# Projections that read the recurrence's output in its own column order, without ACT's copy sorted by tile

## The reference

```
xn = layernorm(x)
# branch 1, a gated linear recurrence
xc    = causal_conv(xn, 4 taps) + conv_b
r, i  = sigmoid(xc @ W_r.T + b_r), sigmoid(xc @ W_i.T + b_i)
a     = sigmoid(log_a) ** (8 r)
h_t   = a_t * h_(t-1) + sqrt(clip(1 - a_t^2)) * i_t * xc_t     # along the 256 tokens
o     = h @ W_out.T
att   = o * rsqrt(mean(o^2) + 1e-6) * gamma
# branch 2, a mixture of 8 experts, each with room for 512 tokens
p, e  = max and argmax of softmax(xn @ Wr);  rank of the token among those of its expert
y     = p * (relu(xn_e @ W1[e]) @ W2[e])        # dropped if the rank is over 511
out   = x + att + y
```

## Time and profile before

| what | value |
|---|---|
| time, median of 3 executions | 130.73 us (130.49 to 130.87) |
| span of the profiled execution, first to last instruction | 128.8 us |
| granted TensorE clock, mean over the span | 0.958 |
| busy: PE, weight loads, DVE, ACT, POOL | 82%, 70%, 79%, 77%, 66% |
| copies sorted by tile on ACT (L796) | 8, together 8.2 us |
| projections (L640) | 64 matmul records, together 8.8 us |

### The profile page before, as it was taken

One profiled execution on the slowest core, in us unless ns is written; L12 is line 12 of the kernel. 1 busy time (PEld: TensorE's weight loads), 2 busy tenths in 40 slices (PEclk: granted clock), 3 DMA queues, 4 the chain that ended last, 5 costly groups with the idle time before them and its releaser, 6 DMA issues.

```text
span 128.8 us, 2229 instructions
## 1 busy us (share of the span) xinstructions
PE 106.2 (82%) x711; PEld 89.9 (70%) x711; DVE 101.8 (79%) x238; ACT 99.6 (77%) x219; POOL 84.6 (66%) x109
## 2 busy tenths in 40 slices
PE   3999999999799999999999997999997999700000
PEld 3999976672379779789879987898697899600000
DVE  5398998999699999979614489999999975973690
ACT  3299792888589589789689999999999799823560
POOL 8987774078788787778777877888787878700000
PEclk9999999999999999999999999999999999998555
DMA  2966964892456365312611711111110111149995
GB/s 85 383 247 173 405 244 173 318 380 66 103 169 181 80 209 139 118 53 56 209 41 41 219 51 41 61 37 41 52 57 25 60 43 61 41 108 302 325 372 215
DMA packets 8234, 19.27 MB, mean 150 GB/s; under 512 B 1689, under 2 KB 1945, under 8 KB 8224
## 3 DMA queue, kind: packets, MB, share of 16 engines
q1 hardware_dynamic: 5424, 13.70, 31.5%
q0 software_dynamic: 2080, 4.19, 11.2%
q10 hardware_dynamic: 720, 1.25, 2.6%
HBM read 10.82 MB, written 8.39 MB: 149 GB/s over the span
## 4 chain that ended last, share of the span: by engine, by line
PE 60%; DVE 9%; DMA 8%; ACT 8%; issue 5%; POOL 4%; POOLq 1%; SPq 1%; DVEq 0%; ACTq 0%
PE bank L624 17%; PE bank L609 6%; PE bank L611 6%; PE bank L610 6%; DMA dec<-y_rows 4%; PE bank L640 4%; PE bank L453 3%; PE bank L561 3%; PE bank L442 3%; POOL xn_tok L405 3%; DMA xn_tok<-xn_rows,idx_in 2%; ACT xc L796 2%; PE bank L594 2%; PE bank L563 2%; PE bank L562 2%
## 5 line engine op out<-in xcount | busy, mean ns | idle before, releaser
L405 POOL DMA_INDIRECT xn_tok<-xn_rows,idx_in x32 | 33.7, 1054 | 14.4 <-issue 9.4
L417 POOL DMA_INDIRECT y_rows<-xn_tok,idx_out x32 | 33.5, 1047 | 9.7 <-issue 9.1
L624 PE MATMUL bank<-w_raw,h_sb 128*128 128x128 f32 x256 | 29.9, 275 | 0.0
L624 PEld LDWEIGHTS bank<-w_raw,h_sb 128*128 128x128 f32 x256 | 29.2, 192 | 0.0
L786 ACT ACTIVATE h_sb<-bank 128x512 f32<-128x512 f32 x32 | 18.8, 598 | 2.5 <-PE bank L611 0.6
L609 PE MATMUL bank<-xg_hi,w_hi 128*128 128x512 f32 x32 | 13.2, 412 | 0.0
L611 PE MATMUL bank<-xg_hi,w_lo 128*128 128x512 f32 x32 | 12.6, 393 | 0.0
L610 PE MATMUL bank<-xg_lo,w_hi 128*128 128x512 f32 x32 | 12.5, 391 | 0.0
L1021 DVE SCALAR_TENSOR_TENSOR xc<-xnT,par,xc 128x1020 f32<-128x1020 f32 (+2 forms) x9 | 11.5, 1277 | 0.3
L640 PE MATMUL bank<-par,xc 128*128 128x128 f32 x64 | 8.8, 280 | 2.2 <-ACT xc L796 1.3
L1061 DVE TENSOR_TENSOR_SCAN xnT<-dec,bank 128x256 f32<-128x256 f32 x16 | 10.1, 674 | 0.3
(11 more groups left out here) (143 smaller groups left out, 243.2 us busy)
## 6 DMA issues: line engine op xcount, KB each, us to landing
w_raw<-in_weights SPq DMA_DIRECT2D x8, 512.0 KB, 3.9
y_rows<-sca SPq DMA_DIRECT2D x4, 512.0 KB, 5.9
dec<-y_rows SPq DMA_DIRECT2D x8, 256.0 KB, 5.7
x_tok<-in_x SPq DMA_DIRECT2D x3, 512.0 KB, 5.9
xn_rows<-xn_tok SPq DMA_DIRECT2D x3, 512.0 KB, 3.6
out<-dec SPq DMA_DIRECT2D x4, 256.0 KB, 3.1
out<-dec ACTq DMA_DIRECT2D x4, 256.0 KB, 2.9
x_tok<-in_x SPq DMA_DIRECT2D x2, 256.0 KB, 3.5
```

The lines of the kernel that those rows point to most:

```text
L405: g.indirect_dma_start(gathered[:, s * D:(s + 1) * D], None, xn_rows, bass.IndirectOffsetOnAxis(ap=idx_in[:, s:s + 1], axis=0)).then_inc(g ...
L417: g.indirect_dma_start(y_rows, bass.IndirectOffsetOnAxis(ap=idx_out[:, s:s + 1], axis=0), gathered[:, s * D:(s + 1) * D], None, bounds_che ...
L624: last = mm(tile_of(e, s), h_sb[:, k * CAP + s * P:k * CAP + (s + 1) * P], w_raw[:, e, F + k * D:F + (k + 1) * D], start=(k == 0), stop=(k ...
```

## The change

ACT's `order` is gone, with its semaphore and the `ordered` buffer. `project` and `fold` read the scan's output `hs` itself. Of each unit's 512 columns, tile i takes every fourth one, from column i on: the stationary operand has a step of 4 fp32 elements, 16 bytes. The matmuls wait for the scan instead of for the copy.

```diff
-        ordered = xc
...
-        ACT_AT = {0: "decay0 gates1", 1: "gates2", 2: "square2 gates3", 3: "scale0", 4: "order0 order1 scale2",
-                  5: "order2 scale3 squares1 order3", 6: "order4 order5 squares3", 7: "squares6 squares7"}
+        ACT_AT = {0: "decay0 gates1", 1: "gates2", 2: "square2 gates3", 3: "scale0", 4: "scale2", 5: "scale3 squares1", 6: "squares3",
+                  7: "squares6 squares7"}
...
-                     5: "lead7 squares2", 6: "order6 order7 squares4 squares5"}
+                     5: "lead7 squares2", 6: "squares4 squares5"}
...
             def project(n):
-                pe.wait_ge(order_done, n + 1)
-                if n in (2, 4):
-                    pe.wait_ge(scan_done, {2: 6, 4: 8}[n])
+                pe.wait_ge(scan_done, {2: 6, 4: 8}.get(n, n + 1))
...
+                by_tile = hs[:, n * HT:(n + 1) * HT].rearrange("d (p i) -> d i p", i=RUN)
                 for i in range(4):
-                    t = 4 * n + i
-                    last = mm(obank[n % 3][:, i * D:(i + 1) * D], ordered[:, t * P:(t + 1) * P],
+                    last = mm(obank[n % 3][:, i * D:(i + 1) * D], by_tile[:, i, :],
                               par[:, WO_T:WO_T + D], start=True, stop=True)
...
+                by_tile = hs[:, n * HT:(n + 1) * HT].rearrange("d (p i) -> d i p", i=RUN)
                 for i in range(4):
-                    t = 4 * n + i
-                    last = mm(FOLDED[n][:, i * D:(i + 1) * D], ordered[:, t * P:(t + 1) * P], wog[:, :],
+                    last = mm(FOLDED[n][:, i * D:(i + 1) * D], by_tile[:, i, :], wog[:, :],
                               start=True, stop=True)
...
-            def order(n):
-                cols = slice(n * HT, (n + 1) * HT)
-                act.wait_ge(scan_done, n + 1)
-                a(ordered[:, cols].rearrange("d (i p) -> d p i", i=RUN),
-                  hs[:, cols].rearrange("d (p i) -> d p i", i=RUN), ACT.Copy).then_inc(order_done, 1)
```

More of the change, by code:

```diff
@@ L241, in rglru_moe_kernel @@
         scan_done = sem("scan_done")
-        order_done = sem("order_done")
         o_mm = sem("o_mm")
@@ L823, in _ @@
             names = {"gates": gates, "decay": decay, "lead": lead, "scale": scale, "squares": squares,
-                     "order": order, "square": square}
+                     "square": square}
             for e in range(E):
```

## The result

The changed kernel takes 132.12 us (median of 20; 130.80 to 132.99), the kernel before, run beside it, 130.62 (130.02 to 131.96). The ratio is **1.0097, between 1.0070 and 1.0123**: 1.3 us slower. The prediction was 130.7 us, no change, with a range up to 131.6.

What follows compares the result with a forecast made beforehand. POOL's queue of gathers and scatters was taken to bound the kernel, with the copies on neither path. Span 128.8 + 0 (copies) + 0 (waits) + 0 (step) = 128.8, plus 1.9 around it: 130.7 us, range 130.2 to 131.6.

Steps and rivals of the forecast that it cites:

- the slack: At the last expert's first scatter: PE and DVE could be 1.06 us later before POOL's queue would wait.
- the price of the stationary operand with a step: In the weight loads of `project` and `fold`: reading columns 16 bytes apart costs nothing, term 0.
- the 80 ns pair: Earlier trace's fp16 loads, columns 64 bytes apart, with small matmuls: 80 ns each, under the fp32 pair's 117, so step hidden.
- the high end: Upper price of the step: 71 ns more per load, or 85 by ratio; end cost 0 or 0.1 us.
- The rule against the change: Skill page on 16-byte SBUF lines: fewer than two hits a line pays, so the step pays; no size given.
- that rival's condition: Rival 1's case: the penalty for a new line equals the length of the access, giving 131.6 us.
- Rival 1: `project(2)` to `project(5)`: stepped loads double, pair 0.23 us, PE outruns POOL's slack, 131.6 us; chance 0.16.
- G: What a group of 8 stepped loads gains in length: 0.57 us at 71 ns, 0.68 at 85, 0.9 in rival 1.
- 4G - 1.65: Rival 1's lateness of `down(7)`: 1.95 us at its G of 0.9; 3.4 at G = 1.26.
- The chain at its word: Rival 2: PE bounds, its waits before `project(0)`, `project(4)` and in `up(6)` go, 1.75 us faster, 129.0; chance 0.04.
- POOL's pace: Rival 3: DVE's shifted products hit other scatters, 0.37 us each, 130.3 or 131.1 us; chance 0.06, half each way.
- the clock: Rival 4: PE idles about 1 us before the sixth scan, its clock falls to 1.2 GHz, up to 133.2 us; chance 0.02.

Runs made afterwards that it cites:

- the test: Changed kernel with groups of test products at PE's end, one column step each: fp32 113 ns a pair contiguous, 232 four apart; fp16 58 and 63 at 8 and 32.
- the 28 records ahead: Products with fp32 columns 4 apart, put before the test groups behind the changed kernel's work to bring the clock up; weight loads 307 to 330 ns each.
- the first try: Changed kernel with test products added behind its work, several groups at half clock; full-speed fp32 pairs 173 ns at step 3, 232 at 4, 239 at 8, 219 at 16.
- the second: Changed kernel with test products behind its work again, now with 28 records first to raise the clock; fp32 pairs 113 ns contiguous, 118 two apart, 232 four apart.

## Why the prediction was wrong

**The bound and the slack held.** Removing the copies alone changed nothing (0.9976); POOL's queue did bound the kernel before (one scatter less, -1.0 us); DVE's list stayed where it was. The slack, put at 1.06 us with a lead of 0.68 from release to start, is 0.97: in the changed kernel the eviction ends at 107.97 and the scatter starts at 108.74, 0.77 later. The second slack, 0.72 us against DVE at expert 6, I had not seen; the change didn't touch it.

**The step that failed is the price of the stationary operand with a step**: "I take 0, since the row nearest in kind, the 80 ns pair, lies below the fp32 pair", and with it the high end of 71 or 85 ns. Measured: a pair of 232 ns instead of 113, 119 ns more for each load, above both ends. The fp16 rows were the nearest to be had, and their pair of 80 ns came out at 58 to 63 in the test. What I passed over is that an fp16 load isn't an fp32 load at half the bytes: contiguous it needs 30 ns a pair against 113. Its own rows showed it, 97 ns a record; the fp32 records of 192 ns stood on the page beside them. Dividing 80 ns by 128 columns took the fetches to come one after another, 0.63 ns each, where four may run side by side. The Trainium skill, "TensorE: Matmul & The Clock Gate", section "Weight-path perf modes — Fast Weight Load (FWL) and DoubleRow", says that a load of 128 columns of a type other than fp32 is split into four chunks on four paths. The measured factor agrees (232/58 = 4.0); that this is the cause wasn't tried otherwise. DVE's reads the earlier trace rows told nothing of PE's: besides being another engine's, the source of L874 jumps 512 bytes forth and 508 back, so that it comes to the same 16 bytes again at every other element.

**The rule against the change was the right one.** "SBUF Cachelines" of the Trainium skill's "Advanced Engine Details and Errata" asks for two hits on 16 bytes. Step 2 has them and costs 5 ns; step 4 has one and doubles the load. The page has no size; the runs give it, and it was the length I had named as that rival's condition.

**Rival 1, given 0.16, is what happened**, in its place and by its mechanism. G is 0.90 in the trace (2.03 - 1.13), as it had assumed, and its own sum, 4G - 1.65, gives 1.95 us on `down(7)` and, less 1.06, 0.9: 131.6. Measured 1.3, and 1.43 on POOL; the eviction behind `down(7)` is 2.4 us late (107.68 against 105.49, with the 0.2 added). The difference is `project(0)` and `project(1)`, which the sum left out: they make `down(5)` late, so that `project(2)` begins at 89.82, 0.5 us later than before with the 0.2 added, and not with the scan. I had read that stretch as DVE's alone. The kernel that reads only units 2 to 5 with the step lacks just this: 0.98 us on POOL instead of 1.43. The one with the step in units 0, 1, 6 and 7 has it: `project(2)` begins 0.11 us after `xg_lo` of expert 6 (90.67, 90.56), where before it began 0.39 ahead of it (89.50, 89.89).

**The other rivals.** The chain at its word would have given -1.75 us; the copies' removal alone gave -0.3 +- 0.5. POOL's pace did not shift by itself, and the clock in the changed kernel was as before (0.968, was 0.958).

**The remedy.** Nothing tried beats the kernel before: the copies are free on ACT. With two tokens of each tile interleaved instead of four the step would be 8 bytes and the load nearly free, but 0.9976 is already the value of free loads; it wasn't tried.

## What to carry to other kernels

Ahead of a change that moves work from one engine to another, ask who bounds the end and how many tenths of slack the receiving engine has; here a copy of 8 us was free and 0.9 us more for each projection was not. The chain of waits names the last releaser, not the bound: POOL's constant 0.3 us ahead of 61 instructions said more, and an edit that shortens one list in both kernels proved it. How far such an edit can carry is set by the next slack, which can lie elsewhere: here at expert 6 and with DVE. A price for an unknown access must come from a row of the same data type on the same path, or from a test behind the kernel's end, which costs one run.

## What the hardware showed

Two things I had not expected. A stepped fp32 load doesn't follow TensorE's clock: the 28 records ahead, with columns four values apart, took 307 to 330 ns each from end to end and followed one another every 233 ns, (6.61 - 0.33)/27, though the granted clock was at 1.2 GHz (0.50) until about 126 us; at 2.4 GHz (1.00) behind it the group of L681 took 318 to 330 again, every 232. Contiguous fp32 loads did follow it (333 ns in the first try at half clock, 192 in the second at full). Before the clock fell PE had idled for 1.6 us:

```profile
119.79 6.61 PEld L673 LDWEIGHTS bank<-par,xc 128*128 128x128 f32 x28 [1.75 <-issue]
```

```profile
119.90:123.00 3.10, 3.10 (x14) 3.10 (x14) 3.09 (x11) 1.98 (x7) 0.00 (x0) 0.50 0.99 332
127.50:134.00 6.50, 6.50 (x40) 6.50 (x40) 0.00 (x0) 0.00 (x0) 0.00 (x0) 1.00 0.23 89
```

(the last two lines: stretch, its length, busy time of PE, weight loads, DVE, ACT and POOL, then the granted clock). And POOL's indirect transfers took 0.77 us from the release of a waiting one to its start (107.97 to 108.74 above; 107.70 to 108.47 with the step in units 4 and 5), and 0.3 from one to the next where nothing was waited for.
